# A fused decoder kernel: where twelve projections of the next batch stand among the tiles of the feed-forward layer

## The reference

```python
# stage A, the first one: 16 heads of 32, two windows of 512 queries
q, k, v = x @ Wq.T, x @ Wk.T, x @ Wv.T
scores  = q k^T / sqrt(32), masked (window rows against keys from 0), softmax, @ v, @ Wo.T
x = layernorm(x + that)
...
# stage F, the last one: quantised feed-forward, hidden size 2048
h = bit_linear(x, w1)                   # x rounded to 8 bits by row, w1 to -1, 0, 1
h = silu(depthwise_conv1d(h) + conv_b)  # three taps along the sequence
x = layernorm(x + bit_linear(h, w2))    # h rounded to 8 bits by row, w2 to -1, 0, 1
```

## Time and profile before

| | |
|---|---|
| median of 3 runs | 2674.35 us (2672.11 to 2677.51) |
| the profiled execution's own time | 2672.16 us |
| its span in the profile | 2670.2 us |
| TensorE busy | 2362.6 us, 88% |
| VectorE busy | 1578.5 us, 59% |
| ScalarE busy | 1234.4 us, 46% |
| GpSimd busy | 703.3 us, 26% |
| mean granted TensorE clock | 0.982 of full speed |

### The profile page before, as it was taken

How to read it: one execution, slowest core, us unless ns; L and a number is a source line. 1 busy time by engine, 2 the same in 40 slices (tenths; PEclk the granted TensorE clock), 3 DMA queues, 4 the chain that set the end, 5 groups by cost and what they waited for, 6 DMA issues and landing times.

```text
span 2670.2 us, 37049 instructions
## 1 busy us (share of the span) xinstructions
PE 2362.6 (88%) x13016; PEld 1315.4 (49%) x13032; DVE 1578.5 (59%) x3089; ACT 1234.4 (46%) x2842; POOL 703.3 (26%) x1001
## 2 busy tenths in 40 slices
PE   8889999988878999898888999989888899998866
PEld 3555444545455544354546554444454655444343
DVE  4664634468676461547867655065786746515688
ACT  5753311268574422127857431212885733121495
POOL 0002321037301232013820213101480021410266
PEclk9999999999999999999999999999999999999989
DMA  8001100010300200000030111001003010100000
GB/s 293 17 10 55 43 16 32 0 48 9 112 14 10 70 28 16 32 16 32 9 125 2 50 30 28 32 16 48 1 17 117 2 56 23 44 0 1 1 1 32
DMA packets 58989, 99.43 MB, mean 37 GB/s; under 512 B 13365, under 2 KB 13749, under 8 KB 58297
## 3 DMA queue, kind: packets, MB, share of 16 engines
q1 hardware_dynamic: 58808, 97.06, 10.8%
HBM read 88.66 MB, written 8.39 MB: 36 GB/s over the span
## 4 chain that ended last, share of the span: by engine, by line
PE 67%; DVE 20%; ACT 8%; issue 4%; POOL 1%; DMA 0%; DVEq 0%; POOLq 0%; ACTq 0%; SPq 0%
PE psum L378 21%; PE psum L372 18%; DVE neg_max L1054 6%; PE psum L472 3%; PE psum L456 3%; PE psum L522 2%; PE psum L731 2%; PE psum L759 2%; DVE turned L1104 2%; ACT xT L801 2%; DVE f_a L1061 1%; PE psum L664 1%; DVE f_top L1340 1%; PE psum L542 1%; PE psum L593 1%
## 5 line engine op out<-in xcount | busy, mean ns | idle before, releaser
L372 PE MATMUL psum<-xT,weights 128*128 128x512 f32 x1152 | 509.3, 596 | 18.9 <-DMA weights<-in_a_k 10.2
L372 PEld LDWEIGHTS psum<-xT,weights 128*128 128x128 f32 x1152 | 215.0, 191 | 272.2 <-issue 254.0
L378 PE MATMUL psum<-weights,mixed 128*128 128x512 f32 x768 | 337.3, 594 | 3.1 <-DVE mixed L1285 3.1
L778 ACT ACTIVATE prob<-psum,neg_max 128x128 f32<-128x128 f32 (+3 forms) x512 | 265.0, 544 | 98.9 <-DVE neg_max L1054 98.9
L378 PE MATMUL psum<-weights,xT 128*128 128x512 f32 x640 | 289.0, 596 | 2.4 <-DVE recip L1242 1.6
L1378 POOL TENSOR_SCALAR var<-stats 128x1 f32<-128x1 f32 x192 | 61.6, 321 | 805.0 <-DVE stats L1005 805.0
L1054 DVE TENSOR_REDUCE neg_max<-psum 128x1 f32<-128x128 f32 (+3 forms) x512 | 210.9, 481 | 57.9 <-PE psum L461 29.7
L472 PE MATMUL psum<-ident,prob 128*128 128x128 f32 x1280 | 168.2, 274 | 82.9 <-DVE turned L1104 82.9
L1391 POOL TENSOR_TENSOR f_a<-f_a,f_z 128x256 f32<-128x256 f32 x256 | 199.5, 789 | 130.9 <-DVE f_a L1061 125.6
L378 PEld LDWEIGHTS psum<-weights,mixed 128*128 128x128 f32 x768 | 143.1, 190 | 180.1 <-issue 172.9
L1035 DVE TENSOR_TENSOR x<-psum,x 128x512 f32<-128x512 f32 x128 | 88.3, 690 | 223.4 <-PE psum L378 161.4
(11 more groups left out here) (242 smaller groups left out, 4078.1 us busy)
## 6 DMA issues: line engine op xcount, KB each, us to landing
xT<-in_xT SPq DMA_DIRECT2D x8, 1024.0 KB, 6.2
x<-in_x SPq DMA_DIRECT2D x8, 1024.0 KB, 8.1
out<-x SPq DMA_DIRECT2D x16, 512.0 KB, 2.8
weights<-in_a_k SPq DMA_DIRECT2D x4, 1024.0 KB, 5.1
weights<-in_a_q SPq DMA_DIRECT2D x4, 1024.0 KB, 5.0
weights<-in_a_v SPq DMA_DIRECT2D x4, 1024.0 KB, 4.9
w1f<-in_w SPq DMA_DIRECT2D x4, 1024.0 KB, 14.8
w2f<-in_w SPq DMA_DIRECT2D x4, 1024.0 KB, 17.3
```

What stands on the lines that cost most here:

```text
L372: last = mm(bank[:, 0:n], weights[weight][:, c, heads(g)], rhs(c), start=(c == 0), stop=(c == C - 1))
L378: last = mm(bank, lhsT(c), weights[weight][:, c, :], start=(c == 0), stop=(stop and c == C - 1))
L778: last = run(sb["prob"][:, slot, o:o + keys], bank[:, o:o + keys], ACT.Exp, bias=sb["neg_max"][:, n, qc, j:j + 1], accum_out=sb["a_sum"][: ...
```

## The change

The four projections at the first slots stay. Of the other eight, five stand at later slots among the tiles and three go to the finish: slot 73, which is just ahead of `f_scale(3)`, and twice slot 82, which is behind `f_quant(3, 1)` and just ahead of the first `f_part` of the last quarter. Their order stays.

```diff
@@ -223,7 +223,7 @@
                     (10, ("f_unit", 1))):
         at.setdefault(n, []).append(step)
     if b < B - 1:
-        for n, step in zip((2, 3, 5, 6, 14, 21, 30, 37, 46, 53, 62, 69), FIRST_PROJECTIONS):
+        for n, step in zip((2, 3, 5, 6, 16, 26, 36, 46, 56, 73, 82, 82), FIRST_PROJECTIONS):
             at.setdefault(n, []).append(("next", step))
     for n in range(NSUB * M):
         steps += [("f_hidden", *divmod(n, M))] + at.pop(n, [])
```

## The result

The changed kernel takes 2686.12 us in the median of six runs (2683.93 to 2687.91), the kernel before 2674.39 on the same chip (six runs, 2672.11 to 2677.89): ratio 1.0037, 95% interval 1.0027 to 1.0047. It is slower by 11.7 us, where I had forecast 2675.4 and no measurable change, and it lies 4.6 us above the range. The profiled execution took 2687.91 us, 1.8 above the median, with a span of 2685.9 against 2670.2: 15.7 us to explain.

What follows compares the result with a forecast made beforehand. GpSimd, VectorE and TensorE, all nearly full, were taken to bound the later tiles. Tiles -4.8, statistics -1.5, later multiplications +1.0 and last quarter +6.3 gave +1.0 us: 2674.35 to 2675.4, range 2667.5 to 2681.5.

Steps and rivals of the forecast that it cites:

- to the first mark: Stage F tiles before GpSimd's first mark: slot 14 to 16 costs 0.4 us, dropping 21 saves 2.2, per element.
- first to second mark: Stage F tiles between GpSimd's first two marks: slots 26, 36 replacing 30, 37 cost 0.7 us more per element.
- second to third: Stage F tiles between GpSimd's second and third marks: dropping slot 53, keeping 46, saves 1.0 us per element.
- third mark to V: Up to VectorE's eight multiplications, per element: slot 62 +0.15, slot 56 +0.4, statistics -0.5, later start +0.33 us.
- V to the first output: From VectorE's eight multiplications to the last quarter's first `f_out`: slot 82's two projections add 1.7, 1.7, 2.9 us.
- slot 26's term: Tiles: slots 26 and 36 cost 1.1 us each against 1.53 for the old pair; +0.7 per element, bounds 0 and +2.
- G + 7.91: Finish: VectorE's eight multiplications start 7.91 us after GpSimd's last group of multiplications begins, 0.33 later than before.
- the third to the fourth mark: Later stage F tiles: dropping slot 62 costs 0.15 us and adding slot 56 costs 0.4, per element.
- the statistics: Between GpSimd's fourth and fifth marks: its wait for VectorE's statistics goes with slot 62, saving 0.5 us per element.
- The finish: Last quarter starts 8.9 us after VectorE's eight multiplications begin, first output at 15.76, no TensorE idle time before, full clock.
- The slower one: Rival: the tiles give nothing, GpSimd with VectorE pacing them; the finish alone adds 7.3 us, 2681.7; chance 0.17.

Runs made afterwards that it cites:

- after_fill: Changed kernel plus idle matmuls filling two TensorE waits in stage D of every element (two, then one); 2677.97 us, 1.0011 of the kernel before.
- before_late1: Kernel before plus one unread matmul (0.86 us) on TensorE at the end of element 0's stage A; 2677.53 us, ratio 1.0006.
- before_late3: Kernel before plus three unread matmuls (2.6 us) on TensorE at the end of element 0's stage A; 2678.21 us, ratio 1.0013.
- the best slots: Kernel before with its last eight projections at slots 14, 24, 30, 40, 46, 56, 62, 73; 2667.45 us, with stage D's idle times filled 2662.50.

## Why the prediction was wrong, step by step

In sums over elements 0 to 2, each from the marks:

| step | forecast | measured |
|---|---|---|
| to the first mark (14 to 16, 21 gone) | -5.4 | -5.0 |
| first to second mark (26, 36 for 30, 37) | +2.1 | +6.9 |
| second to third (53 gone) | -3.0 | -3.5 |
| third mark to V (56, 62, statistics, V later) | +1.1 | +3.3 |
| V to the first output | +6.3 | +5.1 |
| stages A to E | 0 | +9.2 |

**The step that failed most is one I never wrote: that work which is not moved keeps its time.** Stages A to E gave 9.2 of the 15.7 us between the profiled executions, and by the estimate above some 5 of the 11.7 between the medians. The cause is shown as far as the clock goes: three idle times that both kernels have, the length of every stretch by which of them half speed follows, and a median 8.1 us lower once two are filled.

**The second is slot 26's term, +0.7.** At the full clock my number was right, as far as one element shows: in after_fill's element 1 the pair 26, 36 costs 26.90 - 24.76 = 2.14 us over element 3, and I had 1.53 + 0.7 = 2.23. What I missed is the idle time of 1.21 us ahead of tile 26, behind which half speed can follow, and then hits whatever is put there: another 1.6 us per element. With a projection at slot 26 half speed followed there in 11 of the 12 elements that were profiled; with the slots of before in 3 of 12, always in element 2, where it fell on short work that had time. Those rows were there to see.

**V came later than G + 7.91.** In element 0 it is G + 8.16, 0.25 off; there the copy, the rounding and `f_s2b` stand as forecast. In elements 1 and 2 it is G + 9.03 and nearly the same. Windows of PE in element 1:

```profile
1342.00:1344.00 2.00, 0.60 (x2) 0.50 0.00 0
1344.00:1346.00 2.00, 2.00 (x8) 0.50 0.00 0
1346.00:1348.00 2.00, 2.00 (x7) 0.50 0.00 0
```

Around an idle time of 3.63 us, which element 0 has as well, some 7 us pass at half speed in the place of 3.5, so the last `f_peak` are late. The distance from the third to the fourth mark (+0.53 for a forecast +0.55) and the statistics (-0.52 for -0.5) were right.

**The finish was right.** L756 at V + 8.68 for V + 8.9, the first output at V + 15.35, 15.30 and 15.30 for V + 15.76, at the full clock. It was 0.4 too high: 0.2 in the start, 0.2 in the quarter, which took 6.67 us and not 6.86. The Trainium skill's rule in TensorE: Matmul & The Clock Gate, "What's actually happening" (the throttled clock is the default, activity releases it) fits the direction of this: the filled idle times of stage D had the full clock behind them in all 12 stretches. But an idle time alone does not decide: that of 1.21 us had half speed behind it in one element of after_fill and not in the next.

**The rivals.** The slower one was right on stage F: up to V the three elements lost 1.7 us where I had a gain of 5.2, and with the finish that makes +6.7, for its +7.3. It came out by slot 26's clock, not by GpSimd, and at 2681.7 it still lies 4.4 us short, for it left stages A to E alone as well.

**Open.** What decides whether half speed follows a given idle time. The first element's stage D lies ahead of all that was moved, and its clock differs between the profiled executions; so part of it varies from run to run. That the changed stage F tips the later elements is argued from the traces of the three kernels with its slots (eight of their nine stretches at 510.8 to 511.5, against none of nine in before, before_late1 and before_late3, which begin each stage F at times up to 2.6 us apart) and not shown by a run that sets the clock. That slot 36 in the place of 37, or 16 in the place of 14, is worth anything by itself was not tried alone.

## What to carry to other kernels

Before moving work out of a slot, look for the idle times of TensorE in front of its old and new place: one projection put into one delayed nothing here and had the full clock behind it, and one put right behind another ran at half speed. Let a matmul start where the engine that needs the next tile is in work of its own: moved by two slots, one projection changed the median by 18 us here, 9 of them seen in stage F. And compare the stages that were not touched first: here they held 9.2 of the 15.7 us between the two profiled executions.

## What the runs showed of the hardware

The same idle time of TensorE, 2.16 us ahead of L620, was followed by a clock of 1.00 in one kernel and of 0.54 to 0.60 in the other, at 430 us, in work that is the same in both. A delay of 2.6 us put in at the first element of the kernel before was still there at the last stage F; one of 0.86 us ended at the same place to within 0.1 us, because half speed in the first element's stage B added another 1.6. And three matmuls per element that compute nothing made the kernel before faster by 0.12% (interval 0.03 to 0.22%), the changed one by 8.1 us and the best slots by 5.0 us.
